# A two-stage gated kernel: its opening's loads between the first tiles' rows, and GpSimd's first logits behind a transpose

## The reference

```python
# stage one: one of 4 experts, chosen by the token's id; its three matrices are all ctx_2048[e] (512 x 512)
h = layernorm(x)
g = silu(h @ C[e].T);  u = h @ C[e].T
x = x + tanh(g_xattn) * ((g * u) @ C[e].T)
# stage two: 16 experts of width 352, 2 per token, and a shared one
xt = layernorm(x)
scores = sqrt(softplus(xt @ gate_w.T));  idx = top_2(scores + gate_b);  w = scores[idx] / sum
y = sum_k w_k * W2[e_k] @ (silu(W1[e_k] xt) * (W3[e_k] xt))     # at most 256 tokens per expert
x = x + tanh(g_ffn) * (y + shared_mlp(xt))
```

## Time and profile before

| | |
|---|---|
| median of 3 runs | 484.9 us (484.44 to 484.98) |
| the profiled execution | 489.42 us |
| its span, first to last instruction | 487.6 us |
| TensorE (PE) busy | 463.7 us, 95% of the span |
| VectorE (DVE) busy | 328.8 us, 67% |
| ScalarE (ACT) busy | 256.4 us, 53% |
| GpSimd (POOL) busy | 209.9 us, 43% |
| mean granted clock of TensorE | 0.989 |

### The profile page before, as it was taken

One profiled execution on the slowest core, in us unless ns is written; L12 is line 12 of the kernel. 1 busy time (PEld: TensorE's weight loads), 2 busy tenths in 40 slices (PEclk: granted clock), 3 DMA queues, 4 the chain that ended last, 5 costly groups with the idle time before them and its releaser, 6 DMA issues.

```text
span 487.6 us, 7790 instructions
## 1 busy us (share of the span) xinstructions
PE 463.7 (95%) x2493; PEld 394.6 (81%) x2493; DVE 328.8 (67%) x724; ACT 256.4 (53%) x379; POOL 209.9 (43%) x175
## 2 busy tenths in 40 slices
PE   2879999999999998999999999999999999999993
PEld 1358877888888876888888999999999999999982
DVE  6549988998896834388747776666666666666520
ACT  4834444555554334472344576666666666666531
POOL 0601444555544264452456625444435544442242
PEclk9979999999999999999999999999999999999998
DMA  7825654666756353261539999988869988887545
GB/s 291 283 72 185 205 173 153 195 238 221 253 189 223 108 155 134 71 79 28 76 103 223 251 299 292 279 261 236 260 230 237 281 265 252 259 265 230 109 60 70
DMA packets 29164, 95.02 MB, mean 195 GB/s; under 512 B 4816, under 2 KB 5328, under 8 KB 28624
## 3 DMA queue, kind: packets, MB, share of 16 engines
q0 software_dynamic: 17040, 43.66, 36.5%
q1 hardware_dynamic: 11808, 50.98, 30.4%
q10 hardware_dynamic: 288, 0.01, 0.0%
HBM read 67.50 MB, written 28.70 MB: 197 GB/s over the span
## 4 chain that ended last, share of the span: by engine, by line
PE 85%; DVE 6%; DMA 2%; issue 2%; ACT 1%; POOL 1%; POOLq 0%; another core or an unknown queue 0%; DVEq 0%
PE psG L1275 47%; PE psY L1275 29%; PE psT L1280 6%; DMA ys<-in_x,idx 2%; PE psG L1521 1%; DMA tok_i<-in_ids 1%; DVE xh_sb L903 1%; PE psY L1292 1%; DVE arena L912 1%; DVE arena L908 1%; DVE stats L937 0%; DVE stats L930 0%; DVE gu L919 0%; POOL front L419 0%; POOLq L81 0%
## 5 line engine op out<-in xcount | busy, mean ns | idle before, releaser
L1275 PE MATMUL psY<-arena 128*128 (+1 forms) x372 | 92.2, 398 | 0.0
L1275 PEld LDWEIGHTS psY<-arena 128*128 128x128 f32 x372 | 68.0, 188 | 13.7
L1275 PE MATMUL psG<-arena 128*128 x228 | 59.8, 413 | 4.7 <-DVE arena L912 4.7
L498 POOL DMA_INDIRECT ht<-out,idx x32 | 33.7, 1053 | 65.0 <-PE psT L1280 49.2
L1275 PE MATMUL psY<-slot,arena 128*128 128x512 f32 x240 | 58.9, 395 | 0.0
L1050 DVE TENSOR_TENSOR slot<-raw,slot 128x1536 fp32r<-128x1536 f32 x25 | 43.9, 1757 | 19.7 <-ACT slot L622 18.9
L1275 PEld LDWEIGHTS psG<-arena 128*128 128x128 f32 x228 | 43.2, 195 | 15.0 <-issue 6.5
L1050 DVE TENSOR_TENSOR arena<-raw,arena 128x1536 fp32r<-128x1536 f32 x24 | 42.0, 1757 | 17.2 <-ACT arena L622 17.1
L1275 PEld LDWEIGHTS psY<-slot,arena 128*128 128x128 f32 x240 | 44.2, 188 | 9.4 <-ACT xh_sb L666 0.2
L1275 PE MATMUL psG<-arena,slot 128*128 128x512 f32 x216 | 51.3, 392 | 0.0
L1275 PEld LDWEIGHTS psG<-arena,slot 128*128 128x128 f32 x216 | 40.1, 188 | 8.2
(11 more groups left out here) (228 smaller groups left out, 806.3 us busy)
## 6 DMA issues: line engine op xcount, KB each, us to landing
raw<-in_w SPq DMA_DIRECT2D x51, 768.0 KB
padded<-xh_sb SPq DMA_DIRECT2D x19, 256.0 KB
raw<-in_ctx_t SPq DMA_DIRECT2D x2, 1024.0 KB, 8.7
ht<-in_ctx_t SPq DMA_DIRECT2D x1, 1024.0 KB, 11.6
xh_sb<-in_ctx_t SPq DMA_DIRECT2D x1, 1024.0 KB
out<-log_sb SPq DMA_DIRECT2D x4, 256.0 KB
ht<-out,idx POOLq DMA_INDIRECT x32
xb<-in_x,idx POOLq DMA_INDIRECT x19
```

The costliest lines, as they stand in the source:

```text
L498: pool.indirect_dma_start(ht[:, n, :], None, halves_of_out, slots(e * NA + a, 0)).then_inc(g_here[n], 16)
L1275: ins = pe.matmul(ps, left[a], right[b], start=n == 0 and m == 0, stop=n == total - 1 and m == 2)
```

## The change

SP's load of context 3, with the bias and the zeros behind it, waits for the arrival of tile 2's rows. The three weight pieces are issued one each behind the stores of tiles 1, 2 and 3. On TensorE and ScalarE the second quarter of expert 2's low part moves from step -2 to step -1, where also the third quarter is done; ScalarE makes context 3's high part in step 1. VectorE makes expert 1's low part at the end of step -1, and the two halves of expert 3's in steps 1 and 2. GpSimd's first logits wait until 13 row tiles have been transposed.

```diff
@@ sync
-            sp.wait_ge(first_out, 1)
+            sp.wait_ge(xa_here[2], 16)
             sp.dma_start(ctx_raw(E1 - 1), ctx_t[E1 - 1, :, :]).then_inc(ctx_here[E1 - 1], 16)
...
-            sp.wait_ge(ctx_lo_done, E1)
-            for c in range(3):
-                load(0, c)
-
             for t in range(NT):
                 sp.wait_ge(xh_ready, t + 1)
                 sp.dma_start(padded[t * P:(t + 1) * P, :], xh_sb[:, t % 2, D:2 * D]).then_inc(padded_sent[t % 2], 16)
+                if 1 <= t < 4:
+
+                    sp.wait_ge(ctx_lo_done, E1)
+                    load(0, t - 1)
@@ gpsimd, send_logits
                 pool.wait_ge(rank_idx, 1)
+                if b == 0:
+
+                    pool.wait_ge(bT_ps, 3 * TB + 1)
@@ scalar, step
+                if known == 1:
+                    high_ctx(3)
...
                 if known == -1:
-                    high_ctx(3)
-                if known in (-1, 0):
-                    take_rest(2, known + 3)
+                    take_rest(2, 1)
+                    take_rest(2, 2)
+                if known == 0:
+                    take_rest(2, 3)
...
                 if known == FIRST:
                     take_rest(2, 0)
-                    take_rest(2, 1)
@@ vector
-
-            dve.wait_ge(first_out, 1)
-            link(low_ctx(1, 0, 1))
             dve.wait_ge(tg_ready, 1)
...
                             if pair:
                                 low_h()
-
-                                dve.wait_ge(ctx_lo_done, 1)
-                                dve.nop(nofuse=True).then_inc(ctx_lo_done, 1)
...
-                if known in (0, 1):
-                    if known:
+                if pair:
+
+                    dve.wait_ge(ctx_lo_done, 1)
+                    low_ctx(1, 0, 1).then_inc(ctx_lo_done, 1)
+                if known in (1, 2):
+                    if known == 2:
                         dve.wait_ge(ctx_lo_done, 3)
-                    i = low_ctx(3, known, 2)
-                    if known:
-                        i.then_inc(ctx_lo_done, 1)
+                        low_ctx(3, 1, 2).then_inc(ctx_lo_done, 1)
+
+                        dve.wait_ge(ctx_lo_done, E1)
+                    else:
+                        link(low_ctx(3, 0, 2))
@@ tensor
             rest(2, 0)
-            rest(2, 1)
...
-                if known in (-1, 0):
-                    rest(2, known + 3)
+                if known == -1:
+                    rest(2, 1)
+                    rest(2, 2)
+                if known == 0:
+                    rest(2, 3)
```

## The result

The changed kernel takes **483.46 us** (median of 12 runs, 482.66 to 485.05) where the kernel before takes 485.06 in the same comparison: a ratio of 0.9967, 95% interval 0.9955 to 0.9978. That is 1.6 us faster. The forecast was 479.0, the range ended at 481.2, so the gain is real and the forecast is 4.5 us too low. The profiled execution took 485.05 (span 483.2, mean granted clock 0.993); that of before took 489.42 (span 487.6), so the two traces differ by 4.4 us where the medians differ by 1.6.

What follows compares the result with a forecast made beforehand. TensorE, busy 95% of the span, was taken as the bound. An opening gain of 6.8 us less 0.9 lost on VectorE gave 5.9, subtracted from the median 484.9: 479.0 us, range 476.4 to 481.2.

Steps and rivals of the forecast that it cites:

- The gather of tile 2: Opening: with the last context, bias and zeros held back, tile 2's rows land at 18.6 to 19.5; product possible at 23.0.
- L818 moved: VectorE, opening: expert 1's low half goes behind tile 1 and 2's normalisation, 23.7 to 26.0; no cost, 0.6 us of cover.
- The differences and the clock: TensorE, opening: two differences move behind tile 0's transposes; first product at 23.1, at 2.4 GHz, 3.0 us; gain 6.8 us.
- Rival B: Opening: the first product starts sooner but still runs at the 1.2 GHz level; 481.5 us, from 480.2 if partly; chance 0.13.
- The context's conversion: ScalarE converts the last context in the second tile's step, ending at 31.4; cost zero, up to 0.8 us kept as range.
- The low context half in step 2: VectorE: the second half of the last low context meets a full step 2; 0.9 us lost.
- The weight pieces: SP: first MLP weights loaded singly behind the stores of the second to fourth row tiles, not needed until step 8; zero.
- The logits wait: GpSimd's first logits wait for the thirteenth transpose, four sends ending near 183.8 instead of 181.5; cost zero.
- rival A: GpSimd's first logits sends cause VectorE's gap at 181; moving them saves 2.4 us more, 476.6 us; chance 0.20.

Runs made afterwards that it cites:

- experiment 7: Changed kernel without GpSimd's logits wait: 483.36, 483.11 us; kernel before with only that wait: 485.41, 484.76, 485.25; change without the wait, weight pieces early: 479.69.
- experiment 2: Changed kernel with its three weight pieces issued together in their old place, behind all four contexts: 486.69 us, ratio 1.0036 to the kernel before.
- experiment 1: Changed kernel with its three weight pieces issued together before the store loop, at about 28 us: 479.67 us, ratio 0.9883 to the kernel before.
- experiment 6: Kernel before with one line of the change, the last context's load, bias row and zeros waiting for tile 2's rows: 490.61 us, ratio 1.0018.

## Why the prediction was right and wrong

1. *The gather of tile 2.* Right. Its rows were there by 18.82, when SP's load went out, inside the predicted 18.6 to 19.5. L914 ran at 22.04, and the product could start near 23.
2. *L818 moved.* Right: 23.60 to 25.89, and L921 behind it still waited 1.00 us for its product. Zero, with the 0.6 us of cover predicted and 1.0 found.
3. *The differences and the clock.* Right in place and size: 23.32 against 23.1, 2.91 us against 3.0, the second product at 28.32 against 28.4. Rival B fell: the granted clock is 1.00 from 22.00 through the product. The gain of 6.8 us was read against the profiled execution and is 6.76 against it. Against a usual execution of the kernel before (second product at 34.26, the cold first product 5.12 us and not 5.48) it is 5.9; against the two others of experiment 7 it is 6.0 and 5.4.
4. *The context's conversion.* Right: zero. ScalarE does it from 29.48 to 31.39 with no wait, and the load takes 7.1 us to land (page, DMA issues) where 8.3 was taken. The Trainium skill's fit of "DMA: Bandwidth & Descriptors" (section "Anatomy of one DMA — SWDGE (gpsimd) path"), 4.4 us by estimate, stayed short of it again. That section gives the fit for transfers issued from GpSimd; this load is SP's and had others beside it, so no run here tests the fit.
5. *The low context half in step 2.* Right in kind: the product of step 4 starts 7.01 us behind that of step 3 where 6.43 is usual, so 0.6 is lost instead of 0.9. No run took this move back alone, so its share is read from the place and not measured apart.
6. *The weight pieces.* **This is the step that failed.** The prediction said "Zero": it asked when the pieces are needed (step 8) and how long SP's queue is held (under a microsecond), and both answers were right. It did not ask what the bytes do to the transfers beside them. (By TensorE's steps the last piece went out at the start of step 6, at 64.79, and not in step 5; that had no part in the loss.) A piece delays tile 1's scatter to 8.2 us and tile 3's to 7.1, where the buffers are wanted again after 6.0 and 5.7, and VectorE has no idle time in these steps to take it up. The price: 3.7 us where two kernels that differ in this alone ran side by side (483.36 and 479.69, both without GpSimd's wait, on the fourth chip), 2.2 us on the third chip, and 3.8 us between 483.46 and 479.67, which are from two comparisons. The earlier trace rows already showed VectorE back to back, and the code ahead of L903 shows what it waits for; the sum should have had a bound for it, from zero to the length of a 768 KB transfer per piece.
7. *The logits wait.* Zero, as taken, wherever it was measured. All those measurements are from chips without the pause; for a chip with it, rival A is open, and the traces lean its way. (The end of the four sends, 183.8 in the prediction, should be 183.5: four sends of 0.98 and three pauses of 0.30. Nothing rests on it.)

The sum with step 6 put right, for the chip of the first comparison: 484.9 - 6.8 + 0.6 + 3.8 = 482.5, 1.0 below the measured 483.46. Most of that is a second, smaller mistake: the 6.8 was sized on an execution 4.5 us above the median, and subtracted from the median. With the 5.9 of a usual execution it is 484.9 - 5.9 + 0.6 + 3.8 = 483.4; and with the pieces early, without the 3.8, 479.6, where 479.67 was measured. The forecast's 479.0 was near that for a kernel that the change is not, and partly by luck: 6.8 was too much by 0.9, and 0.9 too much by 0.3. Its spread of 478.2 to 480.2 does not follow from the two terms named for it, 0.2 and 0.8, which give 478.9 to 479.9; either way the measured 483.46 lies outside.

## What to carry to other kernels

A load that nobody needs for a long time is not free where it is issued: ask which short transfers it will stand beside, and which buffer is waiting for those to land. The place for it is the stretch where the DMA share is low and no wait of a full engine hangs on a transfer; here one such stretch of 11 us (share 0.09) lay just ahead of the crowded steps. When a change moves the event that releases a queue's loads (here the last context half, one step later), follow that queue to its new neighbours. And before taking a gain from a profile off a median, compare the profiled execution with the median: part of what it shows may be its own.

## What was not expected of the hardware

- A store of 256 KB, 2.2 us as a median of 19, took 11.20 us with three 768 KB loads issued ahead of it in the same queue (experiment 2). Moving the same loads in time by 14 us was worth 7.0 us of the kernel.
- A single 768 KB load from one engine's queue made an indirect scatter from another's take 8.2 us. Over the three scatters of 41 to 60 us the median is 6.7 us with the loads among them and 3.7 without (experiment 1).
- One program, one input: the kernel before takes 485.2 to 485.4 on three chips and 489.7 and 491.0 on two others. The changed kernel takes 483.2 to 483.5 on either kind. So the same change gains 1.6 to 2.1 us on some chips and 7.8 on another (ratio 0.9839). Why is open. In the one long trace of before (489.42), 2.7 of its 4.5 us above a usual execution are the pause of VectorE at 181 and what follows it, 1.0 is ScalarE's late copy in step 7, and 0.8 is in the opening. Neither pause has a releaser in the traces that explains it. No trace of before was taken on the chips of 489.7 and 491.0 themselves.
- With only the load delayed, 3.4 us of earlier start and 2.5 us of shorter product (experiment 6) came out as nothing: VectorE's wait for the gather ahead of the product became ScalarE's wait for the context behind it.
